# State-space block: the product of du with the spread rows of B, computed on GpSimd in place of VectorE

## What is computed

```python
u = silu(conv(in_proj_w @ hidden) + conv_b)             # 256 channels, 4 batches x 256 steps
x_dbl = x_proj_w @ u                                    # dt_lo (8 rows), Bm (16 rows), Cm (16 rows)
delta = softplus(dt_proj_w @ dt_lo + dt_proj_b)
A = -exp(A_log)                                         # 256 channels x 16 states
def step(state, xs):                                    # over the 256 time steps
    dA = exp(d_t[..., None] * A)
    state = state * dA + (d_t * u_t)[..., None] * B_t[:, None, :]
    y_t = einsum('ben,bn->be', state, C_t)
y = (y + D * u) * silu(z)
```

## Time and profile before

| | us |
|---|---|
| median of three runs | 2208.23 |
| the profiled execution's own time | 2212.03 |
| its span (first to last instruction) | 2210.0 |
| busy in the span: TensorE / VectorE / ScalarE / GpSimd | 1885.6 / 1228.7 / 787.7 / 258.7 |
| the loop of 32 units, from the first product at 200.09 to the start of the last at 342.98 | 142.9 |

### The profile page before, as it was taken

One profiled execution on the slowest core, in us unless ns is written; L12 is line 12 of the kernel. 1 busy time (PEld: TensorE's weight loads), 2 busy tenths in 40 slices (PEclk: granted clock), 3 DMA queues, 4 the chain that ended last, 5 costly groups with the idle time before them and its releaser, 6 DMA issues.

```text
span 2210.0 us, 25454 instructions
## 1 busy us (share of the span) xinstructions
PE 1885.6 (85%) x9078; PEld 1198.9 (54%) x9078; DVE 1228.7 (56%) x2789; ACT 787.7 (36%) x1864; POOL 258.7 (12%) x244
## 2 busy tenths in 40 slices
PE   5684776988669599999898678999998899998698
PEld 3451222555555366666665445555555577777355
DVE  5738998746664444444476685333334666665221
ACT  4215444302342133333344322333333455554111
POOL 2711000000104300000000200000000322220111
PEclk9796877989869799999989889999999999999799
DMA  3001000000442200000000213000002000002210
GB/s 149 1 5 53 0 0 20 1 29 1 188 188 89 96 1 1 1 1 0 4 36 1 100 54 134 0 1 1 0 1 102 15 1 1 1 1 96 85 34 13
DMA packets 17371, 83.13 MB, mean 38 GB/s; under 512 B 3136, under 2 KB 10052, under 8 KB 13152
## 3 DMA queue, kind: packets, MB, share of 16 engines
q1 hardware_dynamic: 11168, 71.35, 8.2%
q0 software_dynamic: 2944, 8.03, 1.2%
q10 hardware_dynamic: 3136, 2.13, 0.3%
HBM read 73.23 MB, written 8.81 MB: 37 GB/s over the span
## 4 chain that ended last, share of the span: by engine, by line
PE 72%; DVE 16%; issue 6%; ACT 3%; POOL 3%; DMA 1%; POOLq 0%; DVEq 0%; SPq 0%; ACTq 0%
PE bank L136 58%; PE bank L141 8%; PE bank L3535 4%; DVE space L795 2%; PE bank L3557 2%; DVE space L784 2%; DVE space L1369 1%; DVE space L3049 1%; DMA space<-in_L_attn 1%; DVE space L178 1%; POOL space L625 1%; POOL space L639 1%; DVE space L272 0%; DVE space L189 0%; ACT space L1551 0%
## 5 line engine op out<-in xcount | busy, mean ns | idle before, releaser
L136 PE MATMUL bank<-space 128*128 128x256 f32 (+16 forms) x6734 | 1453.8, 417 | 73.7 <-ACT space L822 10.3
L136 PEld LDWEIGHTS bank<-space 128*128 128x128 f32 (+7 forms) x6734 | 886.2, 178 | 593.8 <-issue 394.1
L141 PE MATMUL bank<-consts,space 128*128 128x128 f32 (+1 forms) x1602 | 253.5, 299 | 170.7 <-DVE space L189 50.0
L141 PEld LDWEIGHTS bank<-consts,space 128*128 128x128 f32 (+1 forms) x1602 | 201.8, 153 | 236.8 <-issue 123.6
L136 PE MATMUL bank<-space,consts 128*128 128x512 f32 (+2 forms) x150 | 96.2, 769 | 58.5 <-DVE space L790 49.0
L197 POOL TENSOR_TENSOR space<-space,consts 128x4 f32<-128x4 f32 x22 | 24.9, 1132 | 684.8 <-DVE space L184 684.8
L2633 POOL TENSOR_TENSOR space<-space,consts 128x4 f32<-128x4 f32 x64 | 68.6, 1071 | 218.2 <-DVE space L2564 218.2
L2428 ACT ACTIVATE space<-bank,space 128x256 f32<-128x256 f32 x128 | 59.5, 470 | 95.7 <-DVE space L2382 95.7
L2382 DVE TENSOR_REDUCE space<-bank 128x2 f32<-128x512 f32 x64 | 44.1, 688 | 86.9 <-PE bank L136 86.8
L136 PEld LDWEIGHTS bank<-space,consts 128*128 128x128 f32 (+1 forms) x150 | 30.2, 227 | 104.1 <-DVE space L790 70.4
L3535 PE MATMUL bank<-space 128*128 x176 | 80.7, 603 | 3.1 <-DVE space L3685 1.6
(11 more groups left out here) (350 smaller groups left out, 1948.3 us busy)
## 6 DMA issues: line engine op xcount, KB each, us to landing
space<-in_L_ffn SPq DMA_DIRECT2D x13, 2048.0 KB, 11.9
space<-in_L_attn SPq DMA_DIRECT2D x10, 2048.0 KB, 13.4
space<-in_L_xattn SPq DMA_DIRECT2D x4, 2048.0 KB, 10.0
expert_results<-space SPq DMA_DIRECT2D x16, 128.0 KB, 3.6
space<-expert_results SPq DMA_DIRECT2D x8, 256.0 KB, 4.7
space<-in_L_xattn SPq DMA_DIRECT2D x1, 1919.0 KB, 19.8
space<-in_L_xattn SPq DMA_DIRECT2D x1, 1536.0 KB, 6.2
space<-in_L_attn SPq DMA_DIRECT2D x1, 1074.5 KB, 4.9
```

What stands on the lines that cost most here:

```text
L136: return self.nc.tensor.matmul(out, lhsT, rhs, start=first, stop=last, skip_group_check=True)
L141: return self.nc.tensor.transpose(out, src, eye)
```

## The change

The products du * B of all 32 units leave VectorE's list and become GpSimd's, at the end of its list for the stage. A new signal `driven` tells VectorE that a unit's `db` is ready for its scan. The wait for `summed(t - 3)` moves with the product, so GpSimd may run up to four units ahead, as far as the ring `db` allows; the wait of the scan for VectorE's own steps goes away.

```diff
-            c_out=2 * SSM_N, firsts=1, decays=32, scanned=32,
+            c_out=2 * SSM_N, firsts=1, decays=32, driven=32, scanned=32,
...
         for t in range(N + 1):
-            if t < N:
-                n, f = self.UNITS[t]
-                da = self.da[t % 3]
-                e.wait_ge(*s.b_out(2 * n + 2))
-                if t >= 4:
-                    e.wait_ge(*s.summed(t - 3))
-                nc.vector.tensor_tensor(self.db[t % 4], self.du[:, f, :], self.bc[n % 3], ALU.mult).then_inc(*c.v.next())
             if t >= 1:
                 n, f = self.UNITS[t - 1]
                 h = self.db[(t - 1) % 4]
...
             if t < N:
                 h = self.db[t % 4]
                 e.wait_ge(*s.decays(t + 1))
-                e.wait_ge(*c.v.so_far)
-                nc.vector.tensor_tensor_scan(h, da, h, 0.0, ALU.mult, ALU.add).then_inc(*s.scanned.one)
+                e.wait_ge(*s.driven(t + 1))
+                nc.vector.tensor_tensor_scan(h, self.da[t % 3], h, 0.0, ALU.mult, ALU.add).then_inc(*s.scanned.one)
...
                                     ALU.subtract).then_inc(*s.split.one)
+        e.wait_ge(*s.du_ready.all)
+        for u, (n, f) in enumerate(self.UNITS):
+            e.wait_ge(*s.b_out(2 * n + 2))
+            if u >= 4:
+                e.wait_ge(*s.summed(u - 3))
+            nc.gpsimd.tensor_tensor(self.db[u % 4], self.du[:, f, :], self.bc[n % 3], ALU.mult).then_inc(*s.driven.one)
```

## The result

The changed kernel takes 2245.01 us (median of four runs, 2243.81 to 2245.55), the kernel before 2209.06 in the same comparison (2207.6 to 2211.2). The ratio is 1.0161, with a 95% interval of 1.0146 to 1.0176: slower by 36 us. The forecast was 2239, the range 2228 to 2254.

The account below looks back on a forecast made before the run. VectorE was taken to bound the loop; 30 collisions of 1.98 us, 59.4, on VectorE's own 109.3 gave +30.4 us. So 2212.0 + 30.4 = 2242.4, less 3.8 for the median: 2239, range 2228 to 2254.

Parts of the forecast that it names:

- The mechanism: In the loop, VectorE operations with two SBUF inputs and GpSimd's products take turns, one operation each; main case, chance 0.79.
- The taps of the first block: VectorE's operations at line 463, 1.30 us apart alone, 2.24 each beside GpSimd; used to price collisions in the loop.
- The scan: VectorE's scan in each unit, never seen beside GpSimd; taken to collide for its whole 2.28 us.
- Rival B: In the loop only the product with C collides, the scan runs freely; about 2209 us, chance 0.05.
- The terms: Each GpSimd product of 1024 adds 1.98 us to VectorE's row in the loop, bounds 1.80 and 2.35.
- the sum of +30.4: Start of the loop's last product with C moves from 342.98 to 373.4 us, bounds +25 to +41.
- The median: Median of three runs lies 3.8 us below the profiled execution, so 2242.4 becomes 2239.
- The lead: GpSimd's lead over VectorE in the loop, cut by the wait for `summed` to two to three units, not four.
- just in time: Chain from TensorE's spread of B to GpSimd's product: 10.4 us if held by a scan, against two periods, 10.9.
- the even period of 5.43: Time per unit of the changed loop: VectorE's 3.45 us plus 1.98 for GpSimd's product.
- Rival A: No collision in any unit, VectorE keeps its durations, period 3.45 us at best; 2186 us, chance 0.09.
- Rival C: GpSimd is starved, moving only when a scan waits for `driven`; 5.9 us per unit, 2253 us, chance 0.07.

Follow-up runs that it names:

- the control: The fastest version's PSUM operands, order and lead, but du * B computed by VectorE instead of GpSimd: 2214.84 us, ratio 1.0032.
- the fastest version: Changed kernel with decays and C read from PSUM, f as outer loop, B spread and copied one unit earlier: 2176.88 us, ratio 0.9860.

## Why the prediction was right

**The mechanism** held: each engine's operation waits for one of the other's, and the loss is VectorE's. The taps of the first block were the right neighbour for operations that the trace had never shown beside GpSimd; the idle products on GpSimd showed the same on the loop itself, without any other change.

**The scan**, which I had called the uncertain member, collides for its full length: 4.43 against 2.28. Rival B falls, and the kernel with C in PSUM shows what it would have needed: there one of two operations is free of GpSimd, but it is the product.

**The terms.** I had taken 1.98 us per GpSimd product between bounds of 1.80 and 2.35. Measured are 1.97 on the product with C, 2.15 on the scan, 2.07 as the mean of the two lines and 2.09 with idle products. That the two kinds paid about evenly, 16 and 15 times, I had not worked out; on the scan alone the term would have been 0.17 short, on the product right to 0.01, which is luck. With 2.07 for 1.98, 30 times, the sum of +30.4 becomes +33.1, which is what the loop lost. The product with C that waits for its own scan starts 375.21 - 372.90 = 2.31 after it, the figure that I had from the end of the loop before. The loop started 0.9 us earlier than before, which I had not foreseen; it changes nothing in the loop's length.

**The median.** I took 3.8 us off because the profiled execution of before lay that far above its median. I should have asked what it came with. Over the later rounds executions of before last from 2202.28 us at a mean granted clock of 0.927 to 2213.6 at 0.917; the profiled one had 0.917. The changed kernel had 0.914 or 0.915 in all four executions, so it never showed the faster kind, and its profiled execution lies 0.1 from its median. What sets the clock of an execution no run here shows. Those 3.8 us and the 2.7 of the term make the difference between 2239 and 2245. Both misses went the same way, and the range held them.

**The lead** I had wrong. I wrote that the wait for `summed` limits it and that GpSimd works two to three units ahead. When GpSimd started units 4 and 5 at 218.27, VectorE had just started the scan of unit 3. GpSimd never waited for `summed`: 63.6 of its 74.2 idle microseconds were waits for the copies of B [line 847], whose chain I had worked out and called just in time. It was in time; VectorE waited for no product. So the even period of 5.43 that I had in mind exists only as a mean, 5.52. The run with less lead shows that the point did not matter.

**Rival A** (no collision, 2186) was wrong for this kernel, but the version with operands in PSUM is that rival made true: a period of 3.43 against the 3.45 that I had given as its best, and 2177 us. **Rival C** (GpSimd starved) falls with the timeline: VectorE's next operation was ready at once and still let GpSimd in, and no scan waited for `driven`.

## What to carry to other kernels

Before work is moved from VectorE to GpSimd, look at where the inputs lie of everything that VectorE will do meanwhile. In this kernel, where VectorE's operation had two inputs in SBUF and GpSimd's read SBUF, the engines took turns, and a GpSimd product of 128x1024 cost VectorE 2.1 us to save it 1.0; with one of VectorE's inputs in PSUM the same product cost it nothing. The loss is not seen as idle time but as longer durations, so compare an instruction's duration beside and without the other engine, and price the pair from any place of the trace where they already meet.

## What the runs showed of the hardware that was not expected

- A scan whose first input lies in PSUM takes 1209 to 1217 ns on average for 128x512 beside GpSimd's products and is not held up by them. In the control with nothing on GpSimd it took 1254; why it was longer there is open.
- Fills by GpSimd pass beside VectorE at no cost to either (953 ns, 64 of them); a copy costs VectorE 0.78 us where the shortest copy takes 1.03.
- A collision cost the scan and the product with C different amounts in the changed kernel, 2.15 and 1.97. With idle products beside the loop before, all lines showed 2.12 to 2.15. Why the product with C got off cheaper is open; it then waited for its own scan just ahead, and part of GpSimd's turn may have passed in that gap. Other runs fit this: with less lead it also waits for its own scan and pays 1.97, while with half of the products moved the product with B, which starts right behind a scan without waiting for it, takes 3.31 to 3.38 where 1.19 is free, so it pays 2.1 to 2.2. No run was made to settle it.
- TensorE's granted clock over the loop was on average 0.78 of full speed before and after the change, between its two levels of 1.2 and 2.4 GHz. In the fastest version it was 0.81 over the first 30 us of the loop, with TensorE busy for 23.8 of them, and 0.98 over the other 83, with TensorE busy for 70.2. Rival A had counted TensorE at the low clock as a bound of such a loop; it was none, since VectorE waited 2.3 us in all.
